# Layer 4's second normalisation: the inverse root from the residual's variance on POOL, not from new statistics on VectorE

## The chip, the core and the metric

The kernel runs on one core of a Trainium2 chip. The metric is the device time of one execution in microseconds (us), the median of three runs. The engines are TensorE (PE, matmuls; its weight loads are PEld), VectorE (DVE), ScalarE (ACT), GpSimd (POOL) and SyncE (SP, which here only issues DMAs). Each works through its own instruction list in order, and they wait for one another by semaphores.

## The reference, cut to what matters

Two decoder blocks, six sublayers in a row, each followed by a layer normalisation without gain or bias:

```python
def _layernorm(x, axis=-1, eps=1e-05):
    m = jnp.mean(x, axis=axis, keepdims=True)
    v = jnp.var(x, axis=axis, keepdims=True)
    return (x - m) / jnp.sqrt(v + eps)
...
x = _layernorm(x + _L1_xattn_ref(x, ctx_1024, ctx_1024, fside_BxSxS2_0, mask_BxSxS2_ik1, ...), axis=-1)
x = _layernorm(x + _L1_ffn_ref(x, L1_ffn_wg, L1_ffn_w1, L1_ffn_b1, L1_ffn_w2, L1_ffn_b2), axis=-1)
```

x is 8 batches of 256 tokens of 256 numbers. The last sublayer is a mixture of 8 experts, one for each token, with a capacity of 320 tokens an expert. A token that is past the capacity gets nothing from it, so its output is the layer norm of x alone, and x is itself the output of a layer norm.

## The kernel before

The five attention sublayers are numbered 0 to 4, and one batch of one of them is a unit: unit u = 8 * layer + batch, 40 units. Layer 4 is units 32 to 39. `schedule()` writes one order of steps, in which the steps of neighbouring units are interleaved (PLACE gives each step of a unit its slot; LAST_PLACE gives earlier ones to unit 39). Every engine goes through this one list and does its part of each step, so the list sets the order of every queue. After the five layers a second block, `routed_mixture`, does the experts.

What one unit of layer 4 does around the change:

- `w`: PE multiplies by the output weights. `w read`: DVE adds the residual into the tile t (line 1216) and takes its statistics, two BN_STATS (line 1082) and two BN_AGGR (line 1085), which give mean and variance in amv. POOL adds epsilon (line 1411, into ave) and takes the power -0.5 (line 1418, into arstd).
- `scatter` of the unit before: POOL issues two indirect DMAs (line 1489) that put the tokens' rows into the experts' slots. By the slots of the list they stand between that power and the next step.
- `norm`: POOL writes X, the normalised rows (line 1428, two instructions, one for each 128 tokens; tile xb, or last_rows for the eighth batch). For units 38 and 39 (VECTOR_NORMS) DVE does this (line 1325).
- `even`: the statistics of X once more, by DVE (`statistics`, lines 1082 and 1085), then POOL: epsilon, power, the mean times the root (line 1479) and its sign turned (line 1480).
- `xT`, `logits`, `chances`, `rank`: PE transposes X (line 501) and multiplies by the gate, DVE makes the choice of expert and the slot numbers.
- `even rows`: ACT writes scale * X + bias (line 1044), and `out` sends it to the output.

Meanwhile PE makes the scores (lines 630 and 653 for the maxima, 640 and 682 for the exponentials), DVE takes the maxima (line 1173) and multiplies the probabilities by the group matrix (line 1369, for seven of the eight pairs of heads; POOL's line 1466 does the eighth), and PE mixes the values (lines 716 and 720).

`inverse_roots` has a form with `again`, which layers 0 and 1 use: two more instructions on the variance v (lines 1414 and 1415) and one power over three pairs of columns. It gives 1/sqrt(v+e), 1/sqrt((1+e')v + e e') and sqrt(v+e). The product of the last two is the factor of a norm of a norm.

Of the kernel before, what the change touches and what calls it, by code (L numbers as in the profile page):

```python
# [25 lines left out]
ALU = mybir.AluOpType  # L26
ACT = mybir.ActivationFunctionType
AX = mybir.AxisListType

P = 128  # L30
B, S, C = 8, 256, 256
H, D = 16, 16
CC = C // P
TT = S // P
# [17 lines left out]
FFN, CTX = 2, 3  # L52
# [157 lines left out]
def attention_layers(nc, outer, ctx, t, known, slots_dram, shared):  # L210
    def sb(name, shape, dt=F32):
        return ctx.enter_context(nc.sbuf_tensor(name, shape, dt))
# [52 lines left out]
    X = [XR[b][:, :, 0:C] for b in range(B)]  # L265
    HN = shared["h"]
# [25 lines left out]
    MV = [sb(f"amv{k}", [P, TT, 2]) for k in range(4)]  # L292
    VE = [sb(f"ave{k}", [P, 3, TT]) for k in range(4)]
    RSTD = [sb(f"arstd{k}", [P, 3, TT]) for k in range(4)]
    RATIO = sb("ratio", [P, B, 2, TT])
    MX = sb("mx", [P, TT, 2, PAIRS])
    MC = sb("mx_blocks", [P, 3, 2, PAIRS])
    MB = sb("max_parts", [P, TT, 2, SHIFT, PAIRS])
# [170 lines left out]
    def evened(u):  # L469

        return (dve_step if u in VECTOR_NORMS else pool_step).at("x", u)
# [419 lines left out]
    def _(act):  # L891
# [91 lines left out]
        for step, u, n in ORDER:  # L983
            l = layer(u)
            if (step, u) == ("q read", 0):
                act.wait_ge(consts_in, 16 * len(EARLY))
            if (step, u) == ("v read", B):
                act.wait_ge(*pool_step.at("constants"))
            if step == "T read" and l > 0:
                if u - 2 in PARTED:  # L990
                    act.wait_ge(*pool_step.at("x low", u - 2))
                read_turned("T", u, HT[u % 2], GAIN.get(l))
            elif step == "TC read":
                read_turned("TC", u, KT[u % 2], ("g2", "b2"))
            elif step == "weight parts":
                kind = "qkv"[n]
                act.wait_ge(*weight_in[kind].at(l))
                act.activation(W_HIGH[kind], WEIGHT_OF[kind][:, :, :], ACT.Copy).then_inc(*act_step("weight high", l, kind))
            elif step == "x high" and u in PARTED:
                act.wait_ge(*xT_in[u % 2].at(u))  # L1000
                if u - 2 in PARTED:
                    act.wait_ge(*bank_filled.at("v", u - 2))
                act.activation(HT_HIGH[u % 2], HT[u % 2][:, :, :], ACT.Copy).then_inc(*act_step("x high", u))
            elif step in ("q read", "k read"):
                read_projected(step[0], u)
            elif step == "v read" and l not in VROW:
                act.wait_ge(*bank_filled.at("v", u))
                if layer(u - RING) in CAUSAL:
                    act.wait_ge(*bank_filled.at("o", u - RING, PAIRS // 2 - 1))
                for tt in range(TT):  # L1010
                    a = act.activation(heads_of(u, tt)[:, :, 0:D],
                                       bank_of("v", u)[:, tt, :].rearrange("p (h d) -> p h d", d=D), ACT.Copy)
                a.then_inc(*act_read("v", u))
            elif step == "sums":
                act.wait_ge(*bank_filled.at("sums", u))
                act.activation(NT, bank_of("sums", u)[:, 0, :], ACT.Sqrt, bias=eps_col[:, :], scale=1.0 / D).then_inc(*act_read("sums", u))
            elif step == "shift":
                if u >= 1:
                    for a in range(2):
                        act.wait_ge(*shift_in[(u - 1) % RING][a].at(u - 1))  # L1020
                act.wait_ge(*bank_filled.at("neg", u))
                act.activation(MT[:, :], bank_of("neg", u)[0:SHIFT * H, 0, :], ACT.Copy)\
                   .then_inc(*act_read("neg", u))
                act.wait_ge(*act_read.at("neg", u))
                act.dma_start(*shift_transfer(u, 0)).then_inc(*shift_in[u % RING][0](u))
            elif step == "exp":
                exponentials(u, n)
            elif step == "exp seed":
                seed_exponents(u, n)
            elif step == "mix read" and (n % 2 == 1 if l < 4 else n in (2, 4, 6, 8)):  # L1030
                n = n if l < 4 else n - 1
                act.wait_ge(*bank_filled.at("o", u, n // 2))
                act.activation(O[:, n // 2, :], bank_of("o", u, n // 2)[:, 0, :], ACT.Copy)\  # L1033
                   .then_inc(*act_read("o", u, n // 2))
            elif step == "xT read":
                if u > 4 * B:
                    act.wait_ge(*bank_filled.at("logits", u - 1))
                read_turned("xT", u, HTF, None)
            elif step == "even rows":
                act.wait_ge(*pool_step.at("even", u))  # L1040
                if u > 4 * B:
                    act.wait_ge(*base_out.at(u - 1))
                for tt in range(TT):
                    a = act.activation(HN[:, tt, :], X[u % B][:, tt, :], ACT.Identity, scale=RSTD[CTX][:, 0, tt:tt + 1],
                                       bias=VE[CTX][:, 2, tt:tt + 1])
                a.then_inc(*act_step("even", u))
            elif step == "chances":
                act.wait_ge(*dve_step.at("logits_sub", u))
                act.activation(GE[:, 2, :, :], GE[:, 0, :, :], ACT.Exp).then_inc(*act_step("chances", u))
            elif step == "yT read" and l > 0:  # L1050
                read_turned("yT", u, YT, None)
            elif step == "Tf":
                act.wait_ge(*cleared.at(3))
                read_turned("Tf", u, HTF, GAIN["f"])
            elif step == "route":
                act.wait_ge(*dve_step.at("gate_sub", u))
                act.activation(GT[:, 1, :, :], GT[:, 0, :, :], ACT.Exp).then_inc(*act_step("gate_exp", u))
            elif step == "e0":
                hidden("e0", u, HID_A, ACT.Gelu, bank_filled.at("down", u - 1, 1) if u % B else None)
            elif step == "e2a":  # L1060
                hidden("e2a", u, HID_B, ACT.Gelu, bank_filled.at("down", u - 1, 3) if u % B else None)
            elif step == "e3a":
                hidden("e3a", u, HID_C, ACT.Gelu, bank_filled.at("down", u - 1, 2) if u % B else None, 1)
            elif step == "e2b":
                hidden("e2b", u, HID_A, ACT.Gelu, bank_filled.at("down", u, 0))
            elif step == "e3b":
                hidden("e3b", u, HID_B, ACT.Gelu, bank_filled.at("e2b", u, 1))
            elif step == "e2c":
                hidden("e2c", u, HID_C, ACT.Gelu, bank_filled.at("e3b", u, 1))
            elif step == "e1a":  # L1070
                hidden("e1a", u, HID_A, ACT.Silu, bank_filled.at("e2c", u, 1))

    @block.vector
    def _(dve):
# [240 lines left out]
        for step, u, n in ORDER:  # L1315
            l, b = divmod(u, B)
# [5 lines left out]
            if step == "norm" and u in VECTOR_NORMS:  # L1322
# [2 lines left out]
                    a = dve.tensor_scalar(X[b][:, tt, :], T[u % 2][:, tt, :], MV[u % 2][:, tt, 0:1], RSTD[u % 2][:, 0, tt:tt + 1],  # L1325
                                          ALU.subtract, ALU.mult)
                a.then_inc(*dve_step("x", u))
            elif step == "even":
                dve.wait_ge(*evened(u))
                if u > 4 * B:  # L1330
                    dve.wait_ge(*pool_step.at("even", u - 1))
                statistics(CTX, X[b], ("even", u), False)
            elif step == "weight parts":
                kind = "qkv"[n]
                dve.wait_ge(*act_step.at("weight high", l, kind))
# [67 lines left out]
    def _(pool):  # L1403
        def then(ins):
            ins.then_inc(*pool_chain())
            pool.wait_ge(pool_chain.sem, pool_chain.count)
# [46 lines left out]
        for step, u, n in ORDER:  # L1453
# [20 lines left out]
            elif step == "even":  # L1474
                if u > 4 * B:
                    pool.wait_ge(*act_step.at("even", u - 1))
                inverse_roots(CTX, ("even", u), eps_n)
                pool.wait_ge(*pool_step.at("rstd", "even", u))
                then(pool.tensor_tensor(VE[CTX][:, 1, :], MV[CTX][:, :, 0], RSTD[CTX][:, 0, :], ALU.mult))
                pool.tensor_scalar(VE[CTX][:, 2, :], VE[CTX][:, 1, :], -1.0, None, ALU.mult)\  # L1480
                    .then_inc(*pool_step("even", u))
            elif step == "scatter":
                if u == 4 * B:
# [58 lines left out]
            elif step == "w read":  # L1542
                if l == 2:
                    inverse_roots(u % 2, (u,), eps_f)
                else:
                    inverse_roots(u % 2, (u,), eps_n, {0: eps_n, 1: eps_f}.get(l))
            elif step == "norm" and u not in VECTOR_NORMS:
                centred(u % 2, u, (u,), l in (0, 1))
            elif step == "normf":
                inverse_roots(FFN, ("f", u), eps_n, eps_n)  # L1550
                centred(FFN, u, ("f", u), True)
# [569 lines left out]
```

## Time and profile before

| | |
|---|---|
| median of 3 runs | 1496.61 us (1493.0 to 1503.61) |
| the profiled execution | 1496.2 us, its span 1494.4 us |
| busy in the span | PE 94%, PEld 72%, DVE 66%, ACT 59%, POOL 37% |
| layer 4's units in the span | about 1090 to 1343 us |
| the experts' block | from 1345 us to the end |

The span is the time from the first to the last instruction of the profiled execution. PE's granted clock has two levels, 1.2 and 2.4 GHz, shown as 0.5 and 1.0 of full speed; its mean here is 0.973. Idle time in front of an instruction is put down to what released it. Only idle time that comes last on every engine is worth anything.

### The profile page before, as it was taken

The page shows a single profiled execution, that of the slowest core. Times are in us where ns is not written, and L with a number is a line of the kernel's source. Part 1 is how long each engine was busy: PE and PEld are TensorE (multiplying, and loading weights), DVE is VectorE, ACT ScalarE, POOL GpSimd, SP SyncE. Part 2 cuts the span into 40 slices and gives each one's busy share as a digit, 9 for nine tenths or more (in the row PEclk, how much of TensorE's full clock was granted, in tenths as well). Part 3 has the DMA queues.
Part 4 walks back from the last instruction along what each step waited for, and adds up shares of the span by engine and source line. Part 5 has one row for each costly group of instructions (what it writes and reads, how often), then busy time and mean ns, then how long its engine had stood idle before and what let it go on. Part 6 is the DMA issues. An engine that isn't in the chain of part 4 may idle for free. (4 is left out here: it accounts for less than half of the span.)

```text
span 1494.4 us, 28973 instructions
## 1 busy us (share of the span) xinstructions
PE 1404.7 (94%) x11060; PEld 1068.8 (72%) x11096; DVE 990.6 (66%) x2109; ACT 875.9 (59%) x1442; POOL 558.4 (37%) x727
## 2 busy tenths in 40 slices
PE   8999999999989999999999999988999999868997
PEld 5666666666668888888888888755655555437997
DVE  4677777776664546455553453686678989856896
ACT  1455566676656656464655646545547767637775
POOL 4246765522430121232222211251324454442766
PEclk9899999999989999999999999999999999988999
DMA  8689776773540321301011010143866644116451
GB/s 160 105 146 185 146 152 126 132 117 48 82 58 2 44 32 26 44 9 43 17 28 44 1 51 2 44 103 84 136 158 111 119 86 67 38 36 209 144 184 58
DMA packets 100248, 126.13 MB, mean 84 GB/s; under 512 B 7900, under 2 KB 90099, under 8 KB 97552
## 3 DMA queue, kind: packets, MB, share of 16 engines
q1 hardware_dynamic: 96496, 118.84, 39.3%
q0 software_dynamic: 2032, 4.24, 0.8%
q8 instruction: 89, 1.46, 0.4%
q10 hardware_dynamic: 1584, 1.20, 0.3%
q14 instruction: 47, 0.39, 0.1%
HBM read 51.10 MB, written 9.51 MB: 41 GB/s over the span
## 5 line engine op out<-in xcount | busy, mean ns | idle before, releaser
L950 ACT ACTIVATE probs<-eslot 128x1024 f32<-128x1024 f32 x188 | 192.6, 1024 | 107.5 <-PE eslot L682 104.1
L1173 DVE TENSOR_REDUCE mx<-mslot 128x4 f32<-128x1024 f32 x128 | 156.4, 1222 | 110.9 <-PE mslot L653 109.6
L1472 POOL TENSOR_SCALAR_AFFINE_SELECT probs<-probs 128x512 f32<-128x512 f32 x128 | 82.5, 645 | 343.5 <-ACT probs L948 342.9
L653 PE MATMUL mslot<-stack 48*128 48x256 f32 (+2 forms) x1110 | 164.9, 334 | 12.3 <-DVE mx L1173 7.1
L653 PEld LDWEIGHTS mslot<-stack 48*128 48x128 f32 (+1 forms) x1110 | 98.3, 188 | 99.3 <-issue 77.4
L1167 DVE TENSOR_REDUCE mx_blocks<-mslot 128x3 f32<-128x384 f32 x214 | 114.7, 554 | 57.8 <-PE mslot L653 42.9
L948 ACT ACTIVATE probs<-eslot 128x512 f32<-128x512 f32 (+1 forms) x256 | 111.7, 490 | 43.0 <-PE eslot L682 42.5
L682 PE MATMUL eslot<-stack 50*128 50x256 f32 (+1 forms) x1264 | 125.1, 275 | 6.5 <-ACT probs L950 3.3
L1411 POOL TENSOR_SCALAR ave<-amv 128x2 f32<-128x2 f32 x64 | 22.7, 354 | 289.1 <-DVE amv L1085 248.3
L697 PE MATMUL bank<-probs,v 128*32 128x256 f32 (+1 forms) x2048 | 126.8, 366 | 1.7 <-ACT slot_rows_sb L973 0.8
L745 PE MATMUL bank<-slot_rows_sb,l 128*128 128x256 f32 x512 | 114.8, 382 | 0.0
L682 PEld LDWEIGHTS eslot<-stack 50*128 50x128 f32 (+1 forms) x1264 | 100.6, 191 | 13.6 <-ACT probs L950 4.6
L745 PEld LDWEIGHTS bank<-slot_rows_sb,l 128*128 128x128 f32 x512 | 96.0, 190 | 13.9
L546 PE MATMUL bank<-hT,slot_rows_sb 128*128 128x256 f32 x416 | 102.2, 387 | 1.2 <-DMA slot_rows_sb<-in_proj 1.2
L1033 ACT ACTIVATE o<-bank 128x256 f32<-128x256 f32 x160 | 61.5, 384 | 62.9 <-PE bank L697 54.2
L697 PEld LDWEIGHTS bank<-probs,v 128*32 128x32 f32 x2048 | 55.6, 111 | 54.0 <-issue 22.5
L745 PE MATMUL bank<-hTf,w 128*128 128x256 f32 x384 | 90.2, 388 | 0.0
L1428 POOL TENSOR_SCALAR xb<-t,amv,arstd 128x256 f32<-128x256 f32 x68 | 89.8, 1328 | 0.8
L973 ACT ACT_TABLE_LOAD x48 | 61.6, 1283 | 44.5 <-PE bank L745 44.4
L546 PEld LDWEIGHTS bank<-hT,slot_rows_sb 128*128 128x128 f32 x416 | 77.8, 193 | 13.0 <-issue 2.1
L1165 DVE TENSOR_TENSOR mslot<-mslot,causal_q 128x256 f32<-128x256 f32 x80 | 34.0, 425 | 69.9 <-PE mslot L653 69.4
L745 PEld LDWEIGHTS bank<-hTf,w 128*128 128x128 f32 x384 | 71.7, 192 | 11.3
(277 smaller groups left out, 3455.4 us busy)
## 6 DMA issues: line engine op xcount, KB each, us to landing
stack<-split SPq DMA_DIRECT2D x192, 256.0 KB
w<-in_w SPq DMA_DIRECT2D x16, 1024.0 KB, 6.1
stack<-split SPq DMA_DIRECT2D x96, 128.0 KB
slot_rows_sb<-in_proj SPq DMA_DIRECT2D x15, 256.0 KB, 4.9
slot_rows<-hTf SPq DMA_DIRECT2D x4, 650.0 KB, 4.6
slot_rows_sb<-slot_rows SPq DMA_DIRECT2D x4, 650.0 KB, 5.2
expert_rows<-slot_rows SPq DMA_DIRECT2D x8, 260.0 KB, 2.6
hT<-in_xT SPq DMA_DIRECT2D x8, 256.0 KB, 9.0
```

Of the source, the lines that this page charges most:

```text
L546: mm = pe.matmul(bank_of(kind, u)[:, co, :], WEIGHT_OF[kind][:, ci, at], src[:, ci, :], start=ci == 0, stop=ci == CC - 1)
L653: mm = pe.matmul(ps[:, first:first + m], queries(u, h, k)[:, qt * P:(qt + 1) * P], keys(u, h, k)[:, 0:m], start=clear, stop=clear or qt == ...
L682: mm = pe.matmul(ps[:, a, kt, q0:S], keys(u, h, k)[:, kt * P:(kt + 1) * P], queries(u, h, k)[:, q0:S], start=l != 4, stop=l != 4 or kt == ...
L697: mm = pe.matmul(ps[32 * j:32 * j + 32, 0, q0:S], values(u, kt, 4 * g + j), PR[:, (2 * g + j // 2) % 4, j % 2, kt, 0:S - q0], start=kt == ...
L745: mm = pe.matmul(ps[:, j, :], w[:, k, o:o + P], src[:, k, :], start=k == 0, stop=k == kc - 1)
L948: e = act.activation(PR[:, k, :, kt, 0:S - kt * P], ps[:, :, kt, kt * P:S], ACT.Exp, scale=0.25)
L950: e = act.activation(PR[:, k, :, :, :].rearrange("p a k q -> p (a k q)"), ps[:, :, :, :].rearrange("p a k q -> p (a k q)"), ACT.Exp, scale ...
L973: act.activation(dst[:, 2 * part:2 * part + 2, :], bank_of(kind, u, part)[:, :, :], func)\
L1167: m = dve.tensor_reduce(MC[:, :, a, p], ps[:, 0:3 * P].rearrange("p (n k) -> p n k", k=P), AX.X, ALU.max)
L1173: dve.tensor_reduce(MX[:, :, :, p].rearrange("p q a -> p a q"), MSLOT[0][:, :, :].rearrange("p a (q k) -> p a q k", q=TT), AX.X, ALU.max)\
L1428: a = pool.tensor_scalar(X[b][:, tt, :], T[u % 2][:, tt, :], MV[k][:, tt, 0:1], RSTD[k][:, 0, tt:tt + 1], ALU.subtract, ALU.mult)
L1472: pool.affine_select(diagonal, diagonal, [[0, 2 * TT], [1, P]], ALU.is_ge, 0.0, base=0, channel_multiplier=-1)\
```

## The change

For the units of layer 4, `w read` now calls `inverse_roots` with `again`, so POOL makes all three roots from the residual's variance. `even` on DVE is gone. `even` on POOL is one product of two of these roots into a new small tile, EVEN. ACT scales by EVEN and adds no bias. The output of the skipped tokens is thus X times a factor, with X's mean taken as zero.

```diff
+    EVEN = sb("even", [P, TT])
...
                 act.wait_ge(*pool_step.at("even", u))
+                act.wait_ge(*evened(u))
                 if u > 4 * B:
                     act.wait_ge(*base_out.at(u - 1))
                 for tt in range(TT):
-                    a = act.activation(HN[:, tt, :], X[u % B][:, tt, :], ACT.Identity, scale=RSTD[CTX][:, 0, tt:tt + 1],
-                                       bias=VE[CTX][:, 2, tt:tt + 1])
+                    a = act.activation(HN[:, tt, :], X[u % B][:, tt, :], ACT.Identity, scale=EVEN[:, tt:tt + 1])
...
-            elif step == "even":
-                dve.wait_ge(*evened(u))
-                if u > 4 * B:
-                    dve.wait_ge(*pool_step.at("even", u - 1))
-                statistics(CTX, X[b], ("even", u), False)
...
             elif step == "even":
                 if u > 4 * B:
                     pool.wait_ge(*act_step.at("even", u - 1))
-                inverse_roots(CTX, ("even", u), eps_n)
-                pool.wait_ge(*pool_step.at("rstd", "even", u))
-                then(pool.tensor_tensor(VE[CTX][:, 1, :], MV[CTX][:, :, 0], RSTD[CTX][:, 0, :], ALU.mult))
-                pool.tensor_scalar(VE[CTX][:, 2, :], VE[CTX][:, 1, :], -1.0, None, ALU.mult)\
+                pool.wait_ge(*pool_step.at("rstd", u))
+                pool.tensor_tensor(EVEN[:, :], RSTD[u % 2][:, 1, :], RSTD[u % 2][:, 2, :], ALU.mult)\
                     .then_inc(*pool_step("even", u))
...
-                    inverse_roots(u % 2, (u,), eps_n, {0: eps_n, 1: eps_f}.get(l))
+                    inverse_roots(u % 2, (u,), eps_n, {0: eps_n, 1: eps_f, 4: eps_n}.get(l))
```

POOL's list for unit 33 (its root, the scatter of unit 32, its norm and its even step; ave, arstd and amv are the small tiles of the root, `even` the new one), before:

```order
L1411 TENSOR_SCALAR ave<-amv 128x2 [waits dve_step]
L1418 TENSOR_TENSOR arstd<-ave,powers 128x2 [waits pool_chain]
L1489 DMA slot_rows<-xb,slot_index 2560x260 [waits dve_step,pool_step,cleared]
L1489 DMA slot_rows<-xb,slot_index 2560x260
L1428 TENSOR_SCALAR xb<-t,amv,arstd 128x256 [waits pool_step]
L1428 TENSOR_SCALAR xb<-t,amv,arstd 128x256
L1411 TENSOR_SCALAR ave<-amv 128x2 [waits dve_step,act_step]
L1418 TENSOR_TENSOR arstd<-ave,powers 128x2 [waits pool_chain]
L1479 TENSOR_TENSOR ave<-amv,arstd 128x2 [waits pool_step]
L1480 TENSOR_SCALAR ave<-ave 128x2 [waits pool_chain]
```

Two instructions more now stand ahead of the scatter and the norm, and the power is six columns wide instead of two; behind the norm one instruction is left of four. The same place of the changed kernel (its line numbers are 4 to 6 lower here):

```order
L1407 TENSOR_SCALAR ave<-amv 128x2 [waits dve_step]
L1410 TENSOR_SCALAR ave<-amv 128x2
L1411 TENSOR_SCALAR ave<-amv 128x2
L1414 TENSOR_TENSOR arstd<-ave,powers 128x6 [waits pool_chain]
L1483 DMA slot_rows<-xb,slot_index 2560x260 [waits dve_step,pool_step,cleared]
L1483 DMA slot_rows<-xb,slot_index 2560x260
L1424 TENSOR_SCALAR xb<-t,amv,arstd 128x256 [waits pool_step]
L1424 TENSOR_SCALAR xb<-t,amv,arstd 128x256
L1474 TENSOR_TENSOR even<-arstd 128x2 [waits pool_step,act_step]
```

DVE's list around the same unit's even step (rs and y are the attention outputs, v the values of a later unit), before:

```order
L1195 TENSOR_TENSOR y<-bank,rs 128x256
L1369 TENSOR_TENSOR probs<-probs,l 128x1024
L1173 TENSOR_REDUCE mx<-mslot 128x2x2
L1082 BN_STATS ast<-xb 128x6 x2
L1085 BN_AGGR amv<-ast 128x2 x2
L1118 TENSOR_TENSOR v<-bank,rows 128x16x16 x2
L1369 TENSOR_TENSOR probs<-probs,l 128x1024
```

The four statistics instructions between the maxima and the values are gone, and nothing else on DVE moves:

```order
L1196 TENSOR_TENSOR y<-bank,rs 128x256
L1365 TENSOR_TENSOR probs<-probs,l 128x1024
L1174 TENSOR_REDUCE mx<-mslot 128x2x2
L1119 TENSOR_TENSOR v<-bank,rows 128x16x16 x2
L1365 TENSOR_TENSOR probs<-probs,l 128x1024
```

## Rows read from the trace of the kernel before

**Rows 1.** Waits, 1140 to 1320 us: waiter, releaser: us in total, times, longest.
```profile
PE bank L501 <- POOL xb L1428: 6.8, 5, 1.4
PE mslot L630 <- DVE mx L1173: 2.9, 5, 1.4
```

**Rows 2.** Timeline of PE: start, duration, instruction [idle before it and releaser].
```profile
1162.23 0.66 PE L501 MATMUL bank<-ident,xb 128*128 128x128 f32 x4
...
1224.69 0.66 PE L501 MATMUL bank<-ident,xb 128*128 128x128 f32 x4 [1.37 <-POOL xb L1428]
...
1237.59 0.50 PE L653 MATMUL mslot<-stack 48*128 48x256 f32 x4
```

**Rows 3.** Timeline of DVE, the same unit.
```profile
1222.33 1.21 DVE L1369 TENSOR_TENSOR probs<-probs,l 128x1024 f32<-128x1024 f32 x1
...
1224.66 0.75 DVE L1082 BATCH_NORM_STATS2 ast<-xb 128x6 f32<-128x256 f32 x2
...
1226.24 0.76 DVE L1118 TENSOR_TENSOR v<-bank,rows 128x256 f32<-128x256 f32 x2 [0.55 <-PE bank L568]
...
1238.13 1.23 DVE L1173 TENSOR_REDUCE mx<-mslot 128x4 f32<-128x1024 f32 x1 [0.71 <-PE mslot L653]
...
1247.49 0.25 DVE L1085 BATCH_NORM_AGGREGATE amv<-ast 128x2 f32<-128x6 f32 x2
```

**Rows 4.** Timeline of POOL, from unit 34's root to unit 35's.
```profile
1216.61 1.10 POOL L1411 TENSOR_SCALAR ave<-amv 128x2 f32<-128x2 f32 x1 [1.85 <-DVE amv L1085]
1217.79 0.71 POOL L1418 TENSOR_TENSOR arstd<-ave,powers 128x2 f32<-128x2 f32 x1
...
1221.11 3.52 POOL L1428 TENSOR_SCALAR xb<-t,amv,arstd 128x256 f32<-128x256 f32 x2
...
1226.97 1.21 POOL L1479 TENSOR_TENSOR ave<-amv,arstd 128x2 f32<-128x2 f32 x1
...
1247.83 1.10 POOL L1411 TENSOR_SCALAR ave<-amv 128x2 f32<-128x2 f32 x1 [1.84 <-DVE amv L1085]
```

**Rows 5.** Timeline of POOL in layer 1: the root with `again`, and the norm.
```profile
309.46 0.19 POOL L1414 TENSOR_SCALAR ave<-amv 128x2 f32<-128x2 f32 x1
309.72 0.21 POOL L1415 TENSOR_SCALAR ave<-amv 128x2 f32<-128x2 f32 x1
310.02 1.35 POOL L1418 TENSOR_TENSOR arstd<-ave,powers 128x6 f32<-128x6 f32 x1
...
312.59 2.44 POOL L1428 TENSOR_SCALAR xb<-t,amv,arstd 128x256 f32<-128x256 f32 x2
```

**Rows 6.** Timelines of POOL and of DVE where a product meets a power.
```profile
1165.22 0.73 POOL L1418 TENSOR_TENSOR arstd<-ave,powers 128x2 f32<-128x2 f32 x1
...
1165.38 1.21 DVE L1369 TENSOR_TENSOR probs<-probs,l 128x1024 f32<-128x1024 f32 x1
```

**Rows 7.** Windows in layer 3: busy us (instructions) of PE, PEld, DVE, ACT, POOL; PEclk; DMA.
```profile
978.20:980.40 2.20, 0.02 (x1) 0.00 (x0) 2.20 (x3) 0.56 (x1) 1.84 (x2) 1.00 0.53 156
981.40:984.80 3.40, 3.40 (x28) 1.72 (x26) 1.56 (x4) 1.28 (x2) 3.40 (x4) 0.50 0.35 94
```

**Rows 8.** PE groups in 981.4 to 984.8, then in 974.8 to 978.2: busy us, mean ns.
```profile
L697 PE MATMUL bank<-probs,v 128*32 128x256 f32 x16 | 1.9, 634 | 0.0
...
L697 PE MATMUL bank<-probs,v 128*32 128x256 f32 x16 | 1.1, 385 | 0.0
```

**Rows 9.** Timelines at layer 4's end: DVE, SP's queue, ACT, PE.
```profile
1331.50 0.74 DVE L1325 TENSOR_SCALAR last_rows<-t,amv,arstd 128x256 f32<-128x256 f32 x2 [1.13 <-POOL arstd L1418]
...
1342.88 0.37 SPq L1677 DMA_DIRECT2D slot_rows_sb<-slot_rows  x1
1343.11 1.09 ACT L1044 ACTIVATE h<-last_rows,ave,arstd 128x256 f32<-128x256 f32 x2 [6.87 <-POOL ave L1480]
1344.23 0.37 SPq L1681 DMA_DIRECT2D out_x<-h  x1
...
1358.09 0.41 PE L1813 MATMUL pbank<-xs_low,w_high 128*128 128x320 f32 x1 [1.35 <-ACT hid_both L1868]
```

## The prediction

> **What bounds the kernel now.** The page's busy shares name PE, but the change touches DVE and POOL only in layer 4, so I read the waits of that stretch first, then PE's timeline for the places of the waits, then DVE's and POOL's for the chain behind them. The reader is to see the following. Between 1140 and 1320 us PE waits five times for POOL's norm, 6.8 us in all, and for DVE's maxima only 2.9 us [rows 1]. One such wait is 1.37 us, in front of the transposes of unit 34's X [rows 2]. Units 33 to 37 have one each; unit 32's transposes start at 1162.23 us without one [rows 2].
>
> The steady unit is a ring of three stretches. PE runs from those transposes (1224.69) to the scores at 1237.59 with hardly a pause [rows 2]. These release DVE's maxima at 1238.13, for which DVE had waited 0.71 us, and from there DVE works through to the statistics at 1247.49 [rows 3]. These release POOL's root at 1247.83, exactly one ring (31.22 us) after the root at 1216.61 [rows 4]. POOL goes on to the norm, 1221.11 plus 3.52 us in unit 34, and 0.06 us after its end PE starts [rows 2, 4]. So POOL's piece from the root to the norm is on the path. DVE's second statistics are not: they start at 1224.66, as PE's transposes do, and behind them DVE waits for PE twice, 0.55 us for the values and 0.71 us for the scores [rows 3].
>
> **Part by part.**
>
> *DVE loses four instructions a unit.* They take from 1224.66 until DVE begins to wait, 1226.24 - 0.55 = 1225.69, about 1.0 us [rows 3], 8 us over eight units. I count nothing. What hides them is DVE's waiting for PE, which itself waited for POOL; without them DVE only waits longer. If that cover were gone, 1.0 us a unit could come back, and that is a rival below. In unit 39 the statistics come after the slot numbers and nothing on the path stands behind them.
>
> *POOL's root gets longer, ahead of the norm.* The two extra instructions move the power from 309.46 to 310.02, by 0.56 us; the power takes 1.35 us where it took 0.71, 0.64 more [rows 4, 5]. Together 1.20 us. Behind it are queued two indirect DMAs and the norm, and PE waits for the norm. Nothing is left to hide it in units 33 to 37, where PE already waits: 5 x 1.20 = 6.0 us. In unit 32 PE is busy with other work when the norm is done, and I count nothing; without that cover it would be 1.2 us more.
>
> The price depends on how the norm meets DVE's product. In layer 1 the norm's two halves take 2.44 us, 1.22 each [rows 5]. In unit 34 the second half is due at 1221.11 + 1.22 = 1222.33, just when a product starts, and the pair takes 3.52 us: the half waited for most of the product's 1.21 us [rows 3, 4]. Moved by 1.20 us, the first half would start at 1222.31, within 0.02 us of that same product. If it is held up as the second half is today, the norm ends 1.2 us later. If it is clearly ahead, it passes, the product runs beside it, and the second half no longer waits: the norm ends only 0.1 us later. The other end is one more product, 1.21 us on top, so 2.4 us. I take 1.20, since in the tie of today POOL is the one held up; the ends, 0.5 and 12 us for the five, stay for the range.
>
> A row bears on this in another way. A product that started 0.16 us into a running power took 1.21 us, as always, and the power 0.73 [rows 6]. So I let the longer power delay no product. The Trainium skill (SBUF — State Buffer, section "Who interferes with whom") says otherwise: a DVE instruction with two SBUF inputs and a GpSimd instruction that reads SBUF shut each other out, and the one that starts first keeps the port for its whole length. The trace agrees where DVE is first (line 1479 took 1.21 us behind a product, [rows 4]) and not where a power is.
>
> *POOL loses three instructions behind the norm.* They are off the path; POOL then has nothing to do until line 1466. Nothing.
>
> *ACT and SP.* The same two activations, without a bias; the added wait on X is met, since the product that it also waits for stands behind the norm on POOL. Nothing queued behind ACT moves.
>
> *Unit 39.* DVE's norm waits 1.13 us for the root today [rows 9], so 1.20 us more lands on everything up to the last scatter and on SP's load of the slots at 1342.88. Against it, the even chain behind the scatter shrinks: ACT's rows began at 1343.11, 6.87 us idle before, and the output followed at 1344.23 [rows 9]. With one instruction instead of four they start at about the same time, and the output goes right behind the later load, at 1342.88 + 1.20 + 0.37 = 1344.5, 0.3 us later. In the experts' block PE has 1.35 us of wait at 1358.09 [rows 9]. Between 0.3 and 1.2 us; I take 0.7.
>
> *TensorE's clock.* This is the part that the list of instructions doesn't show. PE's pauses in units 33 to 37 grow from 1.37 to about 2.6 us. In layer 3 PE paused for 2.2 us (978.20 to 980.40), and from 981.40 the granted clock was 0.50, 1.2 GHz, for 3.4 us [rows 7]. There are three pauses of this length in layer 3, each with such a fall behind it; behind the five pauses of 1.3 to 1.4 us in units 33 to 37 there is none. At the lower level sixteen mixing matmuls take 1.9 us, at the higher 1.1 us [rows 8], so 3.4 us at it cost 3.4 x (1 - 1.1/1.9) = 1.4 us. It falls into PE's own stretch of the ring, so it counts in full. A pause of 2.6 us need not bring it each time; I take 3.5 falls of five, 5.0 us, with 0 and 5 x 2.8 us (a fall twice as long) as the ends.
>
> Sum: 6.0 + 0.7 + 5.0 = 11.7 us on the profiled execution's 1496.2, 1507.9 us. The median of the runs is 0.4 above that execution, so 1508 us.
>
> **The rivals.**
>
> *A, the same without the clock.* The longer pauses leave the clock alone. For it: the five present ones do. Against: the three of 2.2 us. 1496.6 + 6.7 = 1503.3 us.
>
> *B, the norm gets past the product.* Its first half goes ahead in units 34 to 36, at 0.1 us each; with 1.2 in units 33 and 37 and 0.7 at the end that is 3.4 us, and pauses near 1.5 us keep the clock in these three: 1500 us, or 1503 with two falls. For it: the distance is 0.02 us. Against: today's tie goes to DVE. By the skill's rule above the longer power would itself push the product back; then the norm's first half would come first, and the result is this one, 1500 us.
>
> *C, DVE's relief pays.* If the product or the maxima behind the removed statistics were what PE needs next, each of the units 32 to 37 would be 1.0 us shorter, and POOL's root would be met in that time: 1496.6 - 6 = 1490.6, faster. It decides where DVE's waits behind the statistics (0.55 and 0.71 us [rows 3]) are zero. For it: DVE is busy for most of this stretch. Against: those waits, and PE's 2.9 us in all for the maxima [rows 1].
>
> *D, the clock falls for longer.* All five pauses bring falls of 6.8 us, 2.8 us each: 6.7 + 14 = 20.7, 1517 us.
>
> *E, nothing reaches the path.* The ring would have to find 1.2 us elsewhere: 1496.6. PE's wait says no.
>
> **Chances.** The forecast 0.50, A 0.17, B 0.13, C 0.06, D 0.10, E 0.04. The range from 1498 to 1514 holds the forecast's own span (1504 to 1513), A and B; C, E and most of D are left out. About 1% (15 us) is what a measurement of this kernel can tell from no change, since its three runs lie 10 us apart. Over 1511.6 are D and a part of the forecast: slower 0.17. Under 1481.6 there is hardly a case: faster 0.02. Within: 0.81.
>
> **What would show it.** Right: in layer 4 line 1418's six-wide power takes 1.35 us, PE's waits for the norm come to about 2.6 us five times, the ring is 32.4 us without and 33.8 with a fall, and three or four windows of granted clock 0.50 stand between 1190 and 1320 us. Wrong: PE's waits stay at 1.4 (B), they are 2.6 and the clock stays up (A), or PE's waits for line 1173 had been the real ones and the ring is shorter than 31.2 (C). The forecast falls too if a product is delayed by the power, which line 1369's durations would show.

## The result and the profile after

| | before | changed |
|---|---|---|
| median of five runs | 1496.61 us (1489.27 to 1503.61) | 1515.86 us (1506.29 to 1518.99) |
| ratio | | 1.0106 [1.007, 1.0141] |
| the profiled execution | 1496.2, span 1494.4 | 1506.29, span 1504.2 |
| from the root of unit 32 to the end | 338.85 us | 358.04 us |

The changed kernel is slower, by 1.1%. The ratio (with its 95% interval) is the record's own figure and not the quotient of the two medians, which would be 1.0129. By the ratio it is 1512.5 us for a kernel before of 1496.61, 4.5 above the forecast of 1508 and inside the range of 1498 to 1514. The median itself, 1515.86, lies 1.9 us above the range.

The profiled execution of the changed kernel is the fastest of its five runs. Unit 32's root begins at 1146.20 us in it, and at 1155.58 in the profile before, though nothing ahead of that point was changed. So a difference of the two spans (9.8 us) says too little. From unit 32's root to the end it is 358.04 - 338.85 = 19.2 us, which is also the difference of the medians. I use that piece in all that follows.

The waits of the changed kernel, 1140 to 1320 us, answer to [rows 1] (columns as there):

```profile
PE bank L502 <- POOL xb L1424: 14.9, 5, 3.6
PE mslot L631 <- DVE mx L1174: 2.9, 5, 1.4
```

The five waits for POOL's norm went from 6.8 to 14.9 us in all (2.6 us each in units 33 to 35, 3.6 and 3.5 in 36 and 37); those for the maxima are what they were. One ring on POOL, from unit 34's root to unit 35's, answers to [rows 4]:

```profile
1210.14 1.11 POOL L1407 TENSOR_SCALAR ave<-amv 128x2 f32<-128x2 f32 x1 [2.01 <-DVE amv L1086]
1211.31 0.19 POOL L1410 TENSOR_SCALAR ave<-amv 128x2 f32<-128x2 f32 x1
1211.57 0.21 POOL L1411 TENSOR_SCALAR ave<-amv 128x2 f32<-128x2 f32 x1
1211.86 1.36 POOL L1414 TENSOR_TENSOR arstd<-ave,powers 128x6 f32<-128x6 f32 x1
1213.42 1.15 POOL L1483 DMA_INDIRECT slot_rows<-xb,slot_index  x1 [0.19 <-POOL arstd L1414]
...
1215.89 3.52 POOL L1424 TENSOR_SCALAR xb<-t,amv,arstd 128x256 f32<-128x256 f32 x2
1219.39 0.19 POOL L1474 TENSOR_TENSOR even<-arstd 128x2 f32<-128x2 f32 x1
```

The next root begins at 1244.27: a ring of 34.13 us, where it was 31.22. The reader is to see that the norm now starts 5.75 us behind the root's start, not 4.50, and takes the same 3.52 us. PE and DVE behind that norm, the answers to [rows 2] and [rows 3]:

```profile
1219.47 0.67 PE L502 MATMUL bank<-ident,xb 128*128 128x128 f32 x4 [2.62 <-POOL xb L1424]
```

```profile
1215.87 1.21 DVE L1365 TENSOR_TENSOR probs<-probs,l 128x1024 f32<-128x1024 f32 x1
...
1221.88 0.76 DVE L1119 TENSOR_TENSOR v<-bank,rows 128x256 f32<-128x256 f32 x2 [3.66 <-PE bank L569]
...
1226.42 1.23 DVE L1174 TENSOR_REDUCE mx<-mslot 128x4 f32<-128x1024 f32 x1 [2.65 <-PE mslot L654]
```

PE pauses for 2.62 us instead of 1.37. DVE, relieved of its statistics, waits 3.66 us for the values where it waited 0.55. The windows behind that pause (columns as in [rows 7]):

```profile
1220.10:1223.50 3.40, 3.40 (x10) 2.68 (x9) 1.62 (x3) 0.60 (x1) 0.00 (x0) 0.52 0.03 10
1223.50:1226.90 3.40, 3.24 (x33) 1.88 (x33) 0.75 (x2) 1.39 (x4) 0.00 (x0) 1.00 0.00 0
```

The granted clock is at its lower level, 1.2 GHz, from 1220.0 us on, for 3.4 us. Each of the five long pauses has such a fall, from 1185.8, 1220.0, 1254.1, 1284.8 and 1312.1 us; in the profile before there is none in this stretch.

The end of layer 4 and the start of the experts' block, on PE, the answer to [rows 9]:

```profile
1339.84 1.12 PE L502 MATMUL bank<-ident,last_rows 128*128 128x128 f32 x4 [2.73 <-DVE last_rows L1326]
...
1355.45 1.94 PE L1798 MATMUL pbank<-ident,slot_rows_sb 128*128 128x128 f32 x8 [10.34 <-DMA slot_rows_sb<-slot_rows]
...
1366.30 0.41 PE L1807 MATMUL pbank<-xs_low,w_high 128*128 128x320 f32 x1 [2.10 <-ACT hid_both L1862]
```

```profile
1366.90:1370.30 3.40, 3.40 (x15) 3.36 (x15) 3.40 (x6) 2.79 (x7) 1.06 (x2) 0.52 0.35 117
```

PE waits 2.10 us for ACT where it waited 1.35, and a sixth fall follows.

### The profile page after: what moved, and what is told of

Its sections match the earlier page's. It is cut to its first block and busy times, and to the rows that moved or that the text cites. A ratio compares the mean times of both kernels' runs of the same rounds, so it can differ in the third digit from the quotient of the medians.

```text
span 1504.2 us, 28927 instructions
## 1 busy us (share of the span) xinstructions
PE 1404.9 (93%) x11060; PEld 1067.8 (71%) x11096; DVE 983.2 (65%) x2077; ACT 875.1 (58%) x1442; POOL 553.2 (37%) x719
## 5 line engine op out<-in xcount | busy, mean ns | idle before, releaser
L1407 POOL TENSOR_SCALAR ave<-amv 128x2 f32<-128x2 f32 x56 | 19.2, 342 | 276.9 <-DVE amv L1086 236.2
```

## The experiments

The theory after this reading: POOL's longer piece ahead of the norm sets the ring, the pauses bring the falls, and DVE's relief is worth nothing. Its rivals: the removals do harm or good of their own; the added length counts in some other way than in proportion. Times are medians, ratios are to the kernel before on the same chip (1498.09 us for root_only to two_extra, 1497.51 for one_extra and those below it). The ratios are the record's; the quotients of the medians differ from them by up to 0.0024. From each profile, one execution of each kernel, I take three numbers: the rings (root to root, units 32 to 39), the time from the root's start to the norm's end in units 33 to 37, and the falls. These are sums over many rows; their rows for one ring are shown.

| | median us | ratio | ring 34 to 35 | root 32 to root 39 | root to norm's end, units 33 to 37 | falls, units 33 to 37 |
|---|---|---|---|---|---|---|
| before | | 1 | 31.22 | 174.87 | 8.03, 8.02, 8.00, 7.98, 7.19 | 0 |
| changed | 1515.86 | 1.0106 | 34.13 | 190.61 | 9.27, 9.27, 9.23, 10.25, 9.28 | 5 |
| root_only | 1507.75 | 1.0064 [1.0038, 1.009] | 34.17 | 187.44 | 9.27, 9.27, 9.24, 9.18, 8.25 | 4 |
| late_roots | 1498.88 | 1.0011 [0.9985, 1.0037] | 31.21 | 174.68 | 8.02, 8.03, 8.00, 7.99, 7.20 | 0 |
| fill | 1505.98 | 1.0052 [1.0027, 1.0077] | 32.45 | 182.76 | 9.26, 9.27, 9.23, 10.25, 9.29 | 0 |
| two_extra | 1512.49 | 1.0084 [1.0054, 1.0114] | 34.15 | 189.83 | 9.27, 9.27, 9.24, 9.11, 8.25 | 4 |
| one_extra | 1509.82 | 1.0069 [1.0039, 1.0099] | 34.15 | 188.65 | 9.27, 9.27, 9.24, 9.12, 8.25 | 4 |
| scatter_late | 1500.13 | 0.9994 [0.996, 1.0029] | 30.50 | 175.36 | 4.73, 4.75, 4.74, 5.53, 4.75 | 2 |
| after_scatter_late | 1493.70 | 0.9959 [0.9932, 0.9986] | 29.77 | 167.73 | 5.75, 5.75, 5.72, 5.65, 5.62 | 1 |
| late_both | 1491.42 | 0.9936 [0.9906, 0.9966] | 29.77 | 167.51 | 4.73, 4.75, 4.75, 5.52, 5.48 | 0 |

### root_only: the added part alone

```diff
-                    inverse_roots(u % 2, (u,), eps_n, {0: eps_n, 1: eps_f}.get(l))
+                    inverse_roots(u % 2, (u,), eps_n, {0: eps_n, 1: eps_f, 4: eps_n}.get(l))
```

Everything else is as before; nobody reads the added roots.

> The kernel before with one part of the change: in layer 4 POOL makes the three roots ahead of the scatter and the norm, and nobody uses the two new ones; VectorE's second statistics and POOL's four-instruction even step stay. Theory (the longer root is the whole change): the ring from root to root is 34.1 us in units 33 and 34 where the kernel before has 31.2, PE's waits for the norm are about 2.6 us, TensorE's clock falls to 0.50 behind each of the five, and the time is 1.0% to 1.3% over the kernel before, as with the full change. Rival (what is removed or replaced does the harm, the missing statistics or the new even step): the ring stays at 31.2 to 32.4 us and the time within 0.5% of before.

It has the whole ring of the changed kernel, 34.17 us, and the same norm's end in units 33 to 35. So the added instructions alone make that ring. The time is only 0.64% over the kernel before, where 1.0% to 1.3% was expected, and there are four falls, not five. In units 36 and 37 it is better than the changed kernel, by 1.07 and 1.03 us. The norm of unit 36 and DVE's rows beside it, first here, then in the changed kernel:

```profile
1284.86 3.52 POOL L1428 TENSOR_SCALAR xb<-t,amv,arstd 128x256 f32<-128x256 f32 x2
```

```profile
1284.88 1.22 DVE L1369 TENSOR_TENSOR probs<-probs,l 128x1024 f32<-128x1024 f32 x1
1286.02 1.21 DVE L1173 TENSOR_REDUCE mx<-mslot 128x4 f32<-128x1024 f32 x1
1288.41 0.75 DVE L1082 BATCH_NORM_STATS2 ast<-xb 128x6 f32<-128x256 f32 x2 [1.17 <-POOL xb L1428]
```

```profile
1280.52 4.53 POOL L1424 TENSOR_SCALAR xb<-t,amv,arstd 128x256 f32<-128x256 f32 x2
```

```profile
1280.48 1.22 DVE L1365 TENSOR_TENSOR probs<-probs,l 128x1024 f32<-128x1024 f32 x1
1281.61 1.22 DVE L1174 TENSOR_REDUCE mx<-mslot 128x4 f32<-128x1024 f32 x1
1282.74 1.22 DVE L1365 TENSOR_TENSOR probs<-probs,l 128x1024 f32<-128x1024 f32 x1
```

The statistics had to wait for the norm, and so kept the next product behind it. With them gone, DVE goes straight on to a product at 1282.74, into the norm's second half, and the norm takes 4.53 us instead of 3.52. So in unit 36 the removed work was a guard. Unit 37 shows the same: root_only's norm takes 2.59 us, with DVE's next product behind the statistics, which waited 2.37 us for it; the changed kernel's takes 3.60, with a product at 1310.05, inside the norm. In unit 36 of root_only there is also a near tie: the norm's first half starts 0.02 us ahead of the product, and yet it takes 2.32 of the 3.52 us, the product its usual 1.22.

### late_roots: the whole change, but the two new roots made behind the norm

```diff
             elif step == "even":
...
+                pool.tensor_scalar(VE[u % 2][:, 1, :], MV[u % 2][:, :, 1], 1.0 + eps_n, eps_n * eps_n, ALU.mult, ALU.add)
+                then(pool.tensor_scalar(VE[u % 2][:, 2, :], MV[u % 2][:, :, 1], eps_n, None, ALU.add))
+                then(pool.tensor_tensor(RSTD[u % 2][:, 1:3, :], VE[u % 2][:, 1:3, :], powers[:, 1:3, :], ALU.pow))
...
-                    inverse_roots(u % 2, (u,), eps_n, {0: eps_n, 1: eps_f, 4: eps_n}.get(l))
+                    inverse_roots(u % 2, (u,), eps_n, {0: eps_n, 1: eps_f}.get(l))
```

(and DVE's next residual waits for this step, since it overwrites the variance.)

> The full change, but the two new roots are made in the even step, behind the norm, by four POOL instructions; the root ahead of the norm is again one instruction and a power two columns wide. VectorE's statistics stay out. Theory: the ring is 31.2 us again, PE's waits are 1.3 to 1.4 us, no fall of the clock between 1150 and 1325 us, time 0.1% to 0.6% under before at most (the tail's even chain) and 1.0% to 1.3% under the full change. Rival (VectorE's relief pays once the root is short): rings of 30.2 us, 6 us or 0.4% under before. Rival (POOL's longer even step collides with VectorE): ring 32 us or more.

Level with before, ratio 1.0011, rings of 31.2 us. The same arithmetic placed behind the norm costs nothing, and DVE's relief of 1.0 us a unit pays nothing: 174.68 against 174.87 us.

### fill: the changed kernel with PE kept busy through the pauses

```diff
...
+                for _ in range(10 if u in range(4 * B + 1, 4 * B + 6) else 0):
+                    pe.matmul(ps.rearrange("p a b -> p (a b)"), ident_b[:, :],
+                              ident_b[:, :].unsqueeze(1).to_broadcast([P, 4, P]), start=True, stop=True)
...
```

> The full change, and PE runs ten matmuls of 512 bf16 columns that nobody reads in front of each wait for the norm in units 33 to 37, into the bank that the transposes then overwrite. Theory (the falls of the clock cost 1.5 us each on top of the longer root): no fall of the clock in these units, rings of 32.5 us instead of 34.1, the five together 7 to 8 us or 0.5% under the full change, still 0.5% over the kernel before. Rival (the falls are a symptom, the ring is set by POOL and VectorE alone): no falls, but rings of 34 us. Rival (the filling delays the transposes): rings over 34 us.

The ten matmuls of unit 34, in front of its transposes, and the window of that ring:

```profile
1223.13 2.33 PE L826 MATMUL bank<-ident_b 128*128 128x512 bf16 x10
1225.82 0.66 PE L831 MATMUL bank<-ident,xb 128*128 128x128 f32 x4 [0.35 <-POOL xb L1431]
```

```profile
1216.46:1248.91 32.45, 31.01 (x282) 18.09 (x284) 26.57 (x48) 21.62 (x30) 14.94 (x13) 1.00 0.50 91
```

POOL's rows are as in the changed kernel (9.27 us to the norm's end), the clock stays at 1.00, and the ring is 32.45 us. This parts the loss up to unit 39's root: 182.76 - 174.87 = 7.9 us are POOL's, 190.61 - 182.76 = 7.85 us are the clock's, 1.6 us a fall. Its rivals (falls without a price, a filling that delays the transposes) both wanted rings of 34 us or more.

### two_extra and one_extra: a smaller dose

The root_only kernel with the narrow power kept (two_extra), then with one of the two small instructions (one_extra):

```diff
                 pool.tensor_scalar(VE[k][:, 1, :], MV[k][:, :, 1], 1.0 + again, eps * again, ALU.mult, ALU.add)
-                a = pool.tensor_scalar(VE[k][:, 2, :], MV[k][:, :, 1], eps, None, ALU.add)
-                n = 3
+                n = 1 if k < 2 and label[0] in range(4 * B, UNITS) else 3
+                if n == 3:
+                    a = pool.tensor_scalar(VE[k][:, 2, :], MV[k][:, :, 1], eps, None, ALU.add)
```

> A half dose: the kernel before, with only the two extra small instructions ahead of layer 4's power, which stays two columns wide; nobody uses their results. They cost 0.56 us. Theory: PE's waits grow to 1.9 us. If pauses of 1.9 us leave the clock alone, rings of 31.8 us, 2.8 us in all, 0.2% over before; if they bring it down as the ones of 2.2 us in layer 3 did, rings of 33.3 us and 0.7% over before. Rival (the norm's place against VectorE's product decides, in steps of 1.2 us): rings of 31.2 us or 32.4 us and nothing between.

I expected 0.56 us to cost 0.56. It cost 1.24 us a unit, as 1.20 did, and that part of the expectation fell; its rival, steps of 1.2 us, stood. POOL and DVE in unit 34 of two_extra:

```profile
1221.03 1.10 POOL L1411 TENSOR_SCALAR ave<-amv 128x2 f32<-128x2 f32 x1 [1.85 <-DVE amv L1085]
...
1222.75 0.71 POOL L1418 TENSOR_TENSOR arstd<-ave,powers 128x2 f32<-128x2 f32 x1
1223.64 1.81 POOL L1489 DMA_INDIRECT slot_rows<-xb,slot_index  x1 [0.18 <-POOL arstd L1418]
```

```profile
1223.23 1.23 DVE L1369 TENSOR_TENSOR probs<-probs,l 128x1024 f32<-128x1024 f32 x1
```

The power took 0.71 us as it should, but the first indirect DMA of the scatter took 1.81. It ends at 1225.45, 0.99 us behind the product's end (1224.46). The same two rows in the kernel before:

```profile
1218.68 1.11 POOL L1489 DMA_INDIRECT slot_rows<-xb,slot_index  x1 [0.18 <-POOL arstd L1418]
```

```profile
1218.81 1.23 DVE L1369 TENSOR_TENSOR probs<-probs,l 128x1024 f32<-128x1024 f32 x1
```

There the DMA begins 0.13 us ahead of the product and takes 1.11 us. In the changed kernel it ends at 1214.57, again 0.99 us behind its product's end (1213.58). That made the theory of a step, tried by one_extra:

> The kernel before with only one small POOL instruction more (a tensor_scalar of 128 x 2, about 0.25 us) ahead of the power of layer 4's units. Theory (a step): in the kernel before the scatter's first indirect DMA is issued 2.07 us after the root begins, 0.13 us ahead of VectorE's next product of probabilities. Anything that pushes it past that start makes it last until 0.98 us after the product's end. So 0.25 us costs as much as 1.20 us did: root to the norm's end 9.27 us in units 33 to 35, PE's pause 2.6 us, falls of the clock, about 1508 us and a ratio near 1.008 to the kernel before. Rival (in proportion): 0.25 us cost 0.25 us, root to norm's end 8.28 us, a pause of 1.6 us, no fall, a ratio of 1.000 to 1.001.

```profile
1219.29 0.19 POOL L1414 TENSOR_SCALAR ave<-amv 128x2 f32<-128x2 f32 x1
1219.55 0.71 POOL L1419 TENSOR_TENSOR arstd<-ave,powers 128x2 f32<-128x2 f32 x1
1220.44 2.09 POOL L1490 DMA_INDIRECT slot_rows<-xb,slot_index  x1 [0.18 <-issue]
```

```profile
1220.31 1.22 DVE L1369 TENSOR_TENSOR probs<-probs,l 128x1024 f32<-128x1024 f32 x1
```

It came as the step said: the DMA, 0.13 us behind the product's start, takes 2.09 us and ends 1.00 us behind the product's end; the norm's end is at 9.27 us, the ring 34.15. One instruction of 0.19 us costs 0.7% of the kernel. The sums to unit 39's root of one_extra and two_extra hold one more fall each, behind unit 37 (from 1337.5 and 1340.9 us), and two_extra's fall in unit 33 is one of 6.8 us, so their sums lie above root_only's.

### The scatter behind the norm

What PE waits for is the norm, and the scatter's two DMAs (2.4 us with their gaps) stand ahead of it. In the placing of the steps:

```diff
+            if step == "scatter" and u < UNITS - 2:
+                n = 39
```

on the kernel before (scatter_late), on the changed one (after_scatter_late) and on late_roots (late_both).

> The kernel before with POOL's scatter of the slot rows moved from between root and norm to behind the norm in units 32 to 37 of layer 4; nothing is removed. Theory (the norm is what PE waits for, and the 2.3 us of the two indirect DMAs lie ahead of it): root to the norm's end falls from 8.0 to about 5.5 us, PE's pause of 1.37 us before the transposes closes, the interval from root to root falls from 31.22 to about 29.8 us, over five units 6 to 7 us: a ratio of about 0.9955. Rival: the norm, moved into the product's time, waits for it there and the DMAs come into the way of the next step, so that the pause stays: a ratio of 1.000 and rings of 31.2 us.

The norm's end came forward even further than expected, to 4.75 us, and PE's pause in front of the transposes is gone. But the ring only fell to 30.50 us, and the time not at all (0.9994): units 36 and 37 gave it back, with two falls behind waits for DVE. The waits of this kernel, 1140 to 1320 us:

```profile
PE bank L845 <- DVE one_hot L1282: 3.2, 3, 1.6
PE mslot L632 <- DVE mx L1175: 1.9, 4, 1.2
```

Now it is DVE's work that PE waits for. One place of it, DVE and then POOL:

```profile
1224.95 1.23 DVE L1175 TENSOR_REDUCE mx<-mslot 128x4 f32<-128x1024 f32 x1 [0.91 <-PE mslot L655]
...
1226.88 2.96 DVE L1187 TENSOR_SCALAR max_parts<-mx 128x32 fp32r<-128x32 f32 x1
```

```profile
1224.98 1.13 POOL L1491 DMA_INDIRECT slot_rows<-xb,slot_index  x1 [0.54 <-POOL ave L1482]
1226.42 0.98 POOL L1491 DMA_INDIRECT slot_rows<-xb,slot_index  x1 [0.30 <-issue]
1227.40 2.39 POOL L1468 TENSOR_TENSOR probs<-probs,l 128x1024 f32<-128x1024 f32 x1
```

A DVE instruction on 32 numbers a partition begins while POOL issues the second DMA and ends (1229.84) only with POOL's product (1229.79). Its usual length in this place is 1.91 us, also to the end of that product; it took 0.17 us in unit 33 of this profile.

> The changed kernel with the same move of the scatter behind the norm in units 32 to 37. Theory: without the DMAs the root and norm end about 7.0 us after the root begins, earlier than the 8.0 us of the kernel before, the pause stays under 1 us, no clock falls in units 33 to 37, rings of 29.8 to 30.3 us, and the time is 4 to 6 us below the kernel before (a ratio of about 0.997), 15 or more below the changed kernel. Rival (the change also costs elsewhere, in the rest of the layer): the ring shortens but the time stays above the kernel before.

Ratio 0.9959, rings of 29.77 us, the norm's end at 5.75 us (7.0 was expected), no waits for DVE's choice of expert, one fall where none was expected. The same move that gave the kernel before nothing takes 22 us from the changed one by the medians (1515.86 to 1493.70, from different rounds).

> The changed kernel with its two new roots behind the norm (as in the kernel that was level with before) and the scatter behind the norm too. If the removal of VectorE's second statistics pays once POOL no longer holds the ring, this is the fastest of all: below scatter_late by up to 1 us a unit, a ratio of 0.992 to 0.995 to the kernel before. If VectorE's relief is worth nothing even then, it is level with scatter_late within 0.2%.

The fastest: 1491.42 us, ratio 0.9936 [0.9906, 0.9966]. POOL, with the roots and the scatter behind the norm:

```profile
1216.14 1.11 POOL L1409 TENSOR_SCALAR ave<-amv 128x2 f32<-128x2 f32 x1 [2.01 <-DVE amv L1088]
1217.34 0.73 POOL L1416 TENSOR_TENSOR arstd<-ave,powers 128x2 f32<-128x2 f32 x1
1218.17 2.72 POOL L1426 TENSOR_SCALAR xb<-t,amv,arstd 128x256 f32<-128x256 f32 x2
...
1223.53 1.14 POOL L1488 DMA_INDIRECT slot_rows<-xb,slot_index  x1 [0.17 <-POOL even L1479]
```

Against scatter_late, which differs by the statistics left on DVE (and the even chain on POOL), the rings are 29.77 to 30.50 us and the sums 167.51 to 175.36. So taking the statistics out does pay, once the scatter no longer holds the norm: 7.85 us, of which the clock's two falls are about 3. But the profiles don't show DVE's saved time as what pays. DVE and then POOL in late_both:

```profile
1228.05 1.23 DVE L1176 TENSOR_REDUCE mx<-mslot 128x4 f32<-128x1024 f32 x1 [1.82 <-PE mslot L656]
...
1229.98 1.91 DVE L1188 TENSOR_SCALAR max_parts<-mx 128x32 fp32r<-128x32 f32 x1
```

```profile
1229.48 2.38 POOL L1464 TENSOR_TENSOR probs<-probs,l 128x1024 f32<-128x1024 f32 x1 [3.54 <-ACT probs L953]
```

Both kernels start these maxima 11.91 us behind unit 34's root (1216.14 here, 1213.04 in scatter_late): the 0.9 us that DVE saved became a longer wait for PE. What differs is POOL. In scatter_late its even chain waited 4.65 us for DVE's statistics, the scatter stands behind that chain, and POOL's product behind the scatter, so the product started 14.36 us behind the root, here 13.34. That makes up the 1.05 us between 2.96 and 1.91. In unit 36, too, DVE reaches the choice of expert 13.3 us behind the root in both, and its instruction on one_hot takes 2.73 us there and 0.17 here. No run moves POOL's scatter alone with the statistics kept, so this is read from the profiles and not tried.

That late_both beats after_scatter_late isn't shown; their intervals overlap and their sums are 0.2 us apart.

## Why the prediction was right, and where it was not

The mechanism was right: slower, by POOL's longer piece ahead of the norm and by the clock behind the longer pauses. The forecast's sum was 11.7 us, measured are 19.2.

- **DVE's four instructions, counted as nothing: right as to gain.** late_roots has the relief and no gain. Not foreseen was that it costs: in units 36 and 37 about 1.0 us each, because the statistics had kept a product out of POOL's way. That is the 2.1 us by which the changed kernel's five norm's ends lie above root_only's.
- **POOL's piece, 5 x 1.20 = 6.0 us: right in size, in part by luck.** root_only measured 1.24, 1.25, 1.24, 1.20 and 1.06, 6.0 us. With the 2.1 us above the changed kernel has 8.1. The norm met the product as the prediction had it: it starts 0.02 us behind the product, and its first half takes 2.30 us of the 3.52. But the price isn't the length of the added instructions. one_extra and two_extra show that for 0.25 and for 0.56 us it is the same 1.24, since the first DMA is caught in a product. The changed kernel's DMA begins only 0.15 us ahead of that product's end and takes 1.15 us, hardly longer than before, so here the length by itself gives the same 1.2. That the length added was just that of the step made the sum come out. Unit 32 cost nothing, as said.
- **The power delays no product: right.** The product at 1212.35 started inside the six-wide power (from 1211.86) and took 1.23 us. The Trainium skill (SBUF — State Buffer, section "Who interferes with whom") has the one that starts first keep the port. The trace agrees for a product ahead of POOL's norm (2.30 us for the half that it met, 1.21 for the other). It disagrees for a power ahead of a product, and in root_only's unit 36, where the norm started 0.02 us ahead of the product and was the one held.
- **Unit 39 and the end, 0.7 us: mis-sized.** Measured are 167.43 - 163.98 = 3.45 us. DVE's norm of unit 39 came 1.2 us later, as said, PE's wait for ACT was 0.75 us longer, and a fall of the clock followed, some 1.5 us. The prediction had no clock in this stretch. The pause there differs between profiles (1.19 to 2.66 us). Why it grows in the changed kernel isn't settled: late_both has 2.66 us without the later norm, and fill, which has the later norm, has 1.19 and no fall, and its stretch is 165.73 us, 1.75 over before.
- **The clock, 3.5 x 1.4 = 5.0 us: mis-sized, the largest miss.** All five pauses brought a fall, at 7.85 us in all, 1.6 each (fill). The length of 3.4 us was right, and the price from 16 matmuls of the mixing a little low. In root_only, one_extra and two_extra four of five pauses had a fall, so 3.5 of five was not far off as a mean, but the three pauses of 2.2 us in layer 3, each with a fall, spoke for five. Two things there were misread or unseen: the third of these falls lasts 6.8 us, not 3.4, and a pause of that kind doesn't always bring one. In the changed kernel's profile the pause of 2.22 us that ends at 975.40 has no fall behind it.

By rings: 31.22 + 1.24 + 1.6 = 34.1 us, against the 33.8 forecast for a ring with a fall. Of the rivals, A (no falls) is refuted by the windows, B (the norm gets past the product) by the norm's 3.52 us and its start 0.02 us behind the product at 1215.87, D (6.8 us falls) by the windows of 3.4 us, E by the ring. C was wrong: DVE's 1.0 us bought nothing in late_roots, nor in ring 34 of late_both, where the same wait for PE takes it up. It was to hold where DVE's waits behind the statistics are zero; they grew instead, to 1.82 us in ring 34 of late_both. B's own argument, the 0.02 us, is answered by root_only's unit 36: there the norm is ahead by that much and is held all the same.

## What to carry to other kernels

Before work is added ahead of an instruction that another engine waits for, look at what is queued between them, and whether it is only just ahead of something on a shared resource; then 0.2 us costs as much as 1.2. Put new small work behind the awaited instruction, and take out of the chain what need not be there (here two DMA issues), before taking load off an engine that waits anyway. If such a relief pays after all, look whether it is the saved time, or only that another engine's queue no longer waits for the removed step. Add to each lengthened pause of PE the fall of its clock, at most in full: of the twenty pauses of 2.4 to 3.6 us in units 33 to 37 of the four kernels here, seventeen had one.

## What was not expected of the hardware

- An indirect DMA's issue on POOL, 1.11 us long, isn't free of DVE: caught by a product it ended 0.99 to 1.00 us behind the product's end, in three kernels (1.81 and 2.09 us long in two of them; 1.15 in the changed one, where it begins only 0.15 us ahead of that end). Begun 0.13 us ahead of a product it took its 1.11 us.
- It seems to work the other way as well: DVE's 128 x 32 instruction, begun in such an issue, took 2.96 us, to the end of the POOL product behind it. In the same profile's unit 33 line 1187's instruction, begun 0.3 us into the issue, took 0.17 us, and the one behind it (line 1188, of the same size), begun 0.5 us into it, 2.95 us, again to the end of POOL's product. One profile shows this; it wasn't tried by itself.
- PE's pauses of 2.45 to 2.62 us in units 33 to 37 had a fall behind four of five in root_only, one_extra and two_extra (one of 6.8 us, the others 3.4); pauses of 1.3 to 1.4 us in front of the transposes had none. But in scatter_late waits of 1.26 and 1.64 us had one each, and after_scatter_late's one fall, from 1287.4, has no pause over 1 us in the 11 us ahead of it. The length of a single pause doesn't tell it alone.
